# Two gated attention and feed-forward layers on one core: the first batch's key blocks made one mixed batch sooner, and the last two row statistics taken inside the second attention's first batch

## The reference

```
x = x + tanh(g_xattn[0]) * _L0_xattn_ref(_layernorm(x), ctx, ctx, mask, ...)   # 32 heads, rotary, capped logits
x = x + tanh(g_ffn[0])   * _L0_ffn_ref(_layernorm(x), ...)                     # base product plus routed low-rank part
x = x + tanh(g_xattn[1]) * _L1_xattn_ref(_layernorm(x), ctx, mask_b, ...)      # second attention
x = x + tanh(g_ffn[1])   * _L1_ffn_ref(_layernorm(x), ...)                     # 2 of 8 experts per row
```

```
scores = einsum('bhdi,bhdj->bhij', qh, kh) / sqrt(dh);  attn = softmax(scores)
o = gelu(einsum('bhij,bhdj->bhdi', attn, vh));          out = Wo @ o + bo
```

## Time and profile before

| | us |
|---|---|
| median of 3 runs (lowest, highest) | 1021.96 (1021.63, 1023.82) |
| profiled execution, own time | 1021.97 |
| its span in the trace | 1020.1 |
| PE busy in the span | 898.2 (88%) |
| DVE busy | 624.2 (61%) |
| ACT busy | 322.0 (32%) |
| POOL busy | 410.9 (40%) |

### The profile page before, as it was taken

How to read it: one execution, slowest core, us unless ns; L and a number is a source line. 1 busy time by engine, 2 the same in 40 slices (tenths; PEclk the granted TensorE clock), 3 DMA queues, 4 the chain that set the end, 5 groups by cost and what they waited for, 6 DMA issues and landing times.

```text
span 1020.1 us, 13788 instructions
## 1 busy us (share of the span) xinstructions
PE 898.2 (88%) x4739; PEld 721.1 (71%) x4739; DVE 624.2 (61%) x1073; ACT 322.0 (32%) x575; POOL 410.9 (40%) x418
## 2 busy tenths in 40 slices
PE   4799999999999899999999999795999998567990
PEld 4677777877877777777877867673888883355770
DVE  5775674375574275575375666485888867856334
ACT  4323133223132123133223133111566666412330
POOL 4462342252441162352162334347665606437540
PEclk9899999999999999999999999897999995669995
DMA  8020020020020020020020020301334205323447
GB/s 297 10 83 1 31 83 1 12 82 2 31 83 1 12 69 14 31 83 1 11 83 1 1 74 1 104 19 43 104 111 146 62 2 213 125 62 124 136 133 267
DMA packets 42446, 70.12 MB, mean 69 GB/s; under 512 B 7240, under 2 KB 14984, under 8 KB 42256
## 3 DMA queue, kind: packets, MB, share of 16 engines
q1 hardware_dynamic: 37264, 56.95, 17.2%
q0 software_dynamic: 3680, 12.06, 3.7%
q10 hardware_dynamic: 1440, 0.24, 0.1%
HBM read 52.59 MB, written 10.22 MB: 62 GB/s over the span
## 4 chain that ended last, share of the span: by engine, by line
PE 78%; DVE 9%; POOL 5%; issue 4%; DMA 2%; ACT 2%; ACTq 1%; SPq 0%; DVEq 0%; POOLq 0%
PE ps L1358 18%; PE ps L1360 17%; PE ps L1359 17%; PE ps L1447 5%; PE ps L1584 4%; PE ps L1455 4%; PE ps L1463 3%; PE ps L1572 2%; PE ps L1565 2%; POOL k_blk L578 1%; DMA rows_in<-h_rows,gather_i 1%; DVE at_lo L1012 1%; ACT at_hi L746 1%; PE ps L1687 1%; PE ps L1538 1%
## 5 line engine op out<-in xcount | busy, mean ns | idle before, releaser
L514 POOL TENSOR_TENSOR q_t<-rot_a,rot_b 128x512 f32<-128x512 f32 x64 | 82.7, 1292 | 146.0 <-DVE rot_b L939 146.0
L1358 PE MATMUL ps<-wo_hi,at_hi 128*128 128x512 f32 x256 | 108.8, 425 | 18.6 <-DVE at_lo L1012 11.9
L937 DVE TENSOR_TENSOR rot_a<-ps,cos 128x512 f32<-128x512 f32 x80 | 55.4, 692 | 113.2 <-PE ps L1360 113.2
L1358 PE MATMUL ps<-xt_hi,wq_hi 128*128 128x512 f32 x256 | 108.3, 423 | 0.2 <-issue 0.2
L1360 PE MATMUL ps<-xt_hi,wq_lo 128*128 128x512 f32 x256 | 101.5, 396 | 0.0
L1359 PE MATMUL ps<-xt_lo,wq_hi 128*128 128x512 f32 x256 | 100.9, 394 | 0.0
L1360 PE MATMUL ps<-wo_hi,at_lo 128*128 128x512 f32 x256 | 100.4, 392 | 0.0
L1359 PE MATMUL ps<-wo_lo,at_hi 128*128 128x512 f32 x256 | 100.0, 390 | 0.0
L746 ACT ACTIVATE at_hi<-ps 128x512 fp32r<-128x512 f32 x64 | 38.2, 597 | 189.1 <-PE ps L1463 189.1
L1017 DVE TENSOR_TENSOR X<-ps,X 128x512 f32<-128x512 f32 x64 | 44.3, 692 | 84.8 <-PE ps L1360 84.8
L735 ACT ACTIVATE ps<-ps 128x512 f32<-128x512 f32 x64 | 37.2, 582 | 176.7 <-PE ps L1447 176.7
(11 more groups left out here) (221 smaller groups left out, 2120.5 us busy)
## 6 DMA issues: line engine op xcount, KB each, us to landing
wq_raw<-in_wq SPq DMA_DIRECT2D x8, 1024.0 KB, 5.4
wo_raw<-in_wo SPq DMA_DIRECT2D x8, 1024.0 KB, 5.1
w_raw<-in_we SPq DMA_DIRECT2D x8, 1024.0 KB, 5.7
y_in<-y_rows SPq DMA_DIRECT2D x16, 256.0 KB, 5.1
X<-in_x SPq DMA_DIRECT2D x4, 512.0 KB, 13.3
wk_raw<-in_wk SPq DMA_DIRECT2D x8, 256.0 KB, 3.0
q_t<-in_ctx_t SPq DMA_DIRECT2D x2, 1024.0 KB, 10.0
wv_raw<-in_wv SPq DMA_DIRECT2D x4, 512.0 KB, 4.1
```

Of the source, the lines that this page charges most:

```text
L514: nc.gpsimd.tensor_tensor(dst, rot_a[:, r % 2, :], rot_b[:, r % 2, :], ALU.add).then_inc(rope_ok, 1)
L937: nc.vector.tensor_tensor(heads(rot_a[:, r % 2, :]), heads(bank), bcast(cos[:, :], 4), ALU.mult)
L1358: nc.tensor.matmul(dst, w_hi, x_hi, start=start and k == 0, stop=False)
```

## The change

It moves four pieces of work and adds or removes no arithmetic.

- POOL makes batch 0's first four key blocks after mixed batch 4 (was 5), and the last four after mixed batch 5 (was 6). `remainder(1)` stays after mixed batch 6.
- POOL's `row_scale(2, 6)` moves behind mixed batch 7.
- DVE's `row_stats(2, 6)` and `row_stats(2, 7)` leave their place ahead of the second attention. They stand now in its first batch, after steps 1 and 2.
- DVE's scaling of the output weights and bias (`wo1g`, `bo1g`) moves from just ahead of the second attention to just behind `mix(1, 1)`.

```
@@ POOL @@
             for b in range(1, B):
                 mixed(b, b % 2)
-                row_scale(2, b - 1, (b - 1) % 2)
+                if b < B - 1:
+                    row_scale(2, b - 1, (b - 1) % 2)
                 if b == B - 5:
                     remainder(0)
+                if b == B - 4:
+                    keys(0, 0, KT)
                 if b == B - 3:
-                    keys(0, 0, KT)
+                    keys(0, KT, H1)
                 if b == B - 2:
-                    keys(0, KT, H1)
                     remainder(1)
+            row_scale(2, B - 2, 0)
             row_scale(2, B - 1, 1)
@@ DVE, batch() @@
                     if u == 1 and more:
                         kept(b + 2, j)
+                    if first and u in (1, 2):
+                        row_stats(2, B - 3 + u, (B - 3 + u) % 2, x2_ok)
@@ DVE, mixed batches @@
             mix(1, 1)
+            nc.vector.tensor_scalar(wo1g[:, :], wo1[:, :], tanh_g[0:E1, 1:2], None, ALU.mult).then_inc(wo1_ok, 1)
+            nc.vector.tensor_scalar(bo1g[:, :], bo1_c[:, :], tanh_g[:, 1:2], None, ALU.mult).then_inc(wo1_ok, 1)
@@
             mixed(B - 1, 1)
-            row_stats(2, B - 2, 0, x2_ok)
-            row_stats(2, B - 1, 1, x2_ok)
             ve.wait_ge(va_ok, CREDIT + 3)
             values(0, 0)
 
-            nc.vector.tensor_scalar(wo1g[:, :], wo1[:, :], tanh_g[0:E1, 1:2], None, ALU.mult).then_inc(wo1_ok, 1)
-            nc.vector.tensor_scalar(bo1g[:, :], bo1_c[:, :], tanh_g[:, 1:2], None, ALU.mult).then_inc(wo1_ok, 1)
             batch(0, 0, first=True)
```

## The result

The changed kernel takes 1013.65 us (median of 4 runs, 1012.60 to 1015.06), the kernel before 1022.13 in the same series; the ratio is 0.991, with a 95% interval of 0.9891 to 0.9929. The forecast was 1013.3. Timed again in two series beside its variants it took 1013.51 us (ratio 0.9883, interval 0.9836 to 0.993) and 1013.90 (0.9921, 0.9899 to 0.9944): 8.2 and 7.7 us under the kernel before of each series, where the first series has 8.5. The profiled execution has a span of 1010.8 us in place of 1020.1.

The account below looks back on a forecast made before the run. It took DVE, waiting on POOL's queue, to bound the handover and PE the attention behind it. -8.97 for the earlier first maximum + 0.32 for the scalings = -8.65 us, from 1021.97 to 1013.3 us; range 1011.6 to 1016.8.

Parts of the forecast that it names:

- What bounds: Handover to second attention: DVE waits for POOL's queue; first maximum at 700.1 in place of 709.07, 8.97 us earlier.
- Key blocks at nothing: POOL before mixed batch 5: four moved blocks (3.99 us) fit the 4.28 us wait, 0.28 over; cost zero.
- The two scalings at 0.32 us: DVE's `wo1g` and `bo1g` in their new place ahead of rows PE waits for: 0.32 us charged, lower end zero.
- The statistics at nothing: Two pairs on DVE in batch 0, where PE bounds: zero charged, other end the full 1.64 us.
- "clock stays up" rival: PE from 700 us at full clock, DVE becomes the bound: about 0.9 us more gain, 1012.4 us; chance 0.09.
- What the sum left out: The sum: -8.97 + 0.32 + 0 + 0 = -8.65 us, an earlier start carried to the end.
- What the statistics hold up: POOL's batch 1 key blocks from 708.9, then SP's copies and ACT's rounding (0.9 us wait): zero charged, bounds 0 and 0.9.
- One sign that I had named as "wrong": New profile: a wait of PE for `k_blk` or `q` copies in batches 1 to 3 would show the forecast wrong.
- The shared port: DVE's `alpha` of mixed batch 6 blocked by POOL's moved key blocks: 0.85 us more by the rule, 1014.2 in all.
- The slower rival: Clock stays at 0.50 through batches 0 and 1: gain gone, 1025 us or more; chance 0.03.

Follow-up runs that it names:

- filler: Extra PE transposes, result never read, in PE's gaps around batch 0: changed kernel with them 1012.49 us; kernel with only the statistics moved, with them, 1017.21 us.

## Why the prediction was right

- **What bounds.** DVE held by POOL's queue for statistics nobody needs yet: right. Both parts together give 8.96 us at the first maximum, where 8.97 were forecast; the key blocks alone give 4.0. One reading was loose and changes nothing: DVE did not stand 6.30 us right behind `t_b`. It waited 0.79 us, took the statistics of batch 6 at 700.39, and then stood 6.30 us for those of batch 7.
- **Key blocks at nothing.** Right, and narrowly: 0.28 us over was forecast and is what is left before mixed batch 5.
- **The two scalings at 0.32 us.** Right: PE's wait at 668 us grew by 0.31, and taking away what stands on that DVE path (the memset, then the scalings) removed the wait.
- **The statistics at nothing.** Right where it was made, at the low clock: 15.05 and 15.07 us with and without them. Not a property of the kernel, though: with the clock up they cost 1.20 us, near the upper end I had kept (1.64).
- **The "clock stays up" rival.** It did not happen, but its arithmetic held. It gave 2.55 us to the full clock and took 1.64 back for the statistics, 0.9 in all. Measured are 2.08 for the clock without statistics (15.07 to 12.99), 1.20 for the statistics, and 0.86 for both together (15.05 to 14.19). Against the first trace (14.34) only 0.15 are left, since there the clock was down for a shorter time.
- **What the sum left out.** It took everything behind the first maximum as it was. The stretch fell from 15.25 us to 14.34, 14.77 and 15.05, by 0.2 to 0.9 us, most where the clock was down shortest. In the first trace this more than makes up for the 0.25 us by which this execution was late at 661 us, so its 9.3 us are more than the 8.65 of the forecast. The medians have 8.5, 8.2 and 7.7 us; that the forecast came within 0.35 us of the median is luck in part, for single runs of the changed kernel differ by more than 2 us.
- **What the statistics hold up.** Right: blocks at 708.73 (708.9 forecast). ACT waited 0.58 us for batch 2's copies (0.9 forecast), DVE 0.47 us behind it, and the first score of batch 2 still came 16.38 us after that of batch 1. Moving the blocks ahead changed nothing. One sign that I had named as "wrong" does stand in the new profile: PE waits 0.76 us at 724.68, in batch 1, and the profile names POOL's `k_blk`. It isn't that. This score needs a block of batch 1, and the last of them was made at 716.75; DVE's subtraction two steps earlier ends at 724.53, and the kernel before has the same wait at the same place, 0.76 us at 733.98, put down to `s_sub`.
- **The shared port.** The row showed the block again: beside the moved key blocks `alpha` of mixed batch 6 took 0.76 us in place of 0.23. By the rule that I had cited from the Trainium skill ("SBUF — State Buffer", Who interferes with whom) this was to be expected, and the trace agrees with it. `lg_n`, which I had not charged, took 0.79 us there, where it is 0.17 to 0.28 elsewhere. As forecast it cost nothing, since `t_b` behind them was on time; but the two took 1.15 us more together, and what hid them was DVE's wait for PE ahead of this `t_b`, gone after the change (692.78) and 1.24 us before it:

```profile
692.22 0.75 DVE L1060 SCALAR_TENSOR_TENSOR t_b<-ps,tanh_g,bbg 128x512 f32<-128x512 f32 x1 [1.24 <-PE ps L1520]
```

- **The slower rival.** Right in kind and too kindly described: the clock can stay down for over 30 us with PE fully busy. I had held against it that it came back behind 5.1 us of full load before. Moving only the statistics shows that this is no safe ground.

What stays open is why the clock comes back behind 3 to 5 us of PE's work in most executions and behind some 30 in the traced long one. In the kernel with the statistics alone 4 of 12 runs were long with filler, in place of 7, and they were shorter, and none came in the kernels with filler and both parts; that is few runs, those with filler were on another chip, and no trace of a long run with filler was taken. So that filler helps against the long runs is not shown.

## What to carry to other kernels

Where a chain runs through an engine's queue, ask of each instruction in front of the waited-for one who needs it and when; here two statistics wanted four batches later held up the whole core for 9 us. Moving work out of an engine's critical place may need the second engine's order moved to match: here the key blocks alone gave under half of the gain, and the statistics alone gave about two thirds of it in five runs of twelve and lost it in the other seven. A gap on PE can cost more than its length: here the steps behind it ran at the lower clock, for 2.2 us in the kernel before. That price hid 1.2 us of DVE's work, so weigh the two terms together. And when one trace is the yardstick for the next expectation, take a second one first: 14.34 us was the shortest of three.

## What had not been expected of the hardware

- A 128x512 normalisation on DVE took 0.54 us with POOL idle and 1.23 beside one subtraction. Beside a row of key blocks (1.0 us each) it took 0.98 us in the kernel before, 1.33 with the key blocks alone moved, and 2.62 in both traces with the statistics alone moved: 2.08 us more than by itself, as long as two blocks and not one. Why it differs is not shown.
- At 0.50 clock PE was busy for 10.00 of 10 us twice over (710 to 730 us) without the clock rising, while in the kernel before it rose behind 5.1 us of full load.
